# Four transformer layers on one core: the softmax of the first attention phase moves from ACT to Pool and behind the transposition

## The reference

```
x = x + L0_xattn(layernorm(x), ctx, ctx, mask0)     # 16 heads of 8, additive mask, relu(ctx @ wo + b)
x = x + L0_ffn(layernorm(x))                        # 8 experts of 512, the best 2 of each token
x = x + L1_xattn(layernorm(x), ctx, ctx, mask1)     # projections with bias, clip to +-100, mask
x = x + L1_ffn(layernorm(x))                        # gated, fake-quantised
x = x + L2_xattn(...); x = x + L2_ffn(...)          # attention; slots with a top-8 routing
x = x + L3_xattn(...); x = x + L3_ffn(...)          # attention with heads of 64; shared and 8 routed experts

scores  = einsum('bhqd,bhkd->bhqk', q, k) + mask
weights = softmax(scores)                           # exp(s - max) / sum
out     = einsum('bhqk,bhkd->bhqd', weights, v)
```

## Time and profile before

| | us |
|---|---|
| median of 3 runs | 2166.7 |
| lowest and highest run | 2157.89, 2175.78 |
| span of the profiled execution | 2161.6 |
| PE, DVE, ACT, POOL busy in the span | 1864.7, 1485.2, 1300.1, 616.4 |

### The profile page before, as it was taken

One profiled execution on the slowest core, in us unless ns is written; L12 is line 12 of the kernel. 1 busy time (PEld: TensorE's weight loads), 2 busy tenths in 40 slices (PEclk: granted clock), 3 DMA queues, 4 the chain that ended last, 5 costly groups with the idle time before them and its releaser, 6 DMA issues.

```text
span 2161.6 us, 49950 instructions
## 1 busy us (share of the span) xinstructions
PE 1864.7 (86%) x17665; PEld 1517.8 (70%) x17669; DVE 1485.2 (69%) x3873; ACT 1300.1 (60%) x4466; POOL 616.4 (29%) x610
## 2 busy tenths in 40 slices
PE   3987988888889999648788989999999998898878
PEld 2776877777778777536666667777787777676765
DVE  5887776786877888566776676776767565564456
ACT  1886655565556688436677766666666654554432
POOL 0003021241312230014343434244353533333221
PEclk9998999999999999867799999999999999999999
DMA  8013334463444310210000011232222223232351
GB/s 240 17 31 102 106 114 144 130 180 96 141 128 140 102 31 7 96 64 20 24 25 2 20 39 33 83 92 66 89 62 80 82 70 105 61 96 79 99 155 51
DMA packets 119637, 178.44 MB, mean 83 GB/s; under 512 B 9824, under 2 KB 77728, under 8 KB 119136
## 3 DMA queue, kind: packets, MB, share of 16 engines
q1 hardware_dynamic: 111712, 159.51, 24.6%
q0 software_dynamic: 7680, 15.74, 2.5%
HBM read 141.26 MB, written 33.95 MB: 81 GB/s over the span
## 4 chain that ended last, share of the span: by engine, by line
PE 37%; DVE 9%; ACT 5%; issue 4%; POOL 1%; DMA 0%; DVEq 0%; ACTq 0%; SPq 0%
PE ps L1659 5%; PE ps L1944 5%; PE ps L1892 3%; PE ps L1697 3%; PE ps L1885 3%; ACT pb L2093 2%; PE ps L1681 2%; PE ps L1866 2%; PE ps L1688 2%; PE ps L1670 2%; PE ps L1707 1%; DVE nm L2472 1%; PE ps L1715 1%; PE ps L1914 1%; PE ps L1858 1%
## 5 line engine op out<-in xcount | busy, mean ns | idle before, releaser
L2093 ACT ACTIVATE pb<-ps,nm 128x128 f32<-128x128 f32 x1024 | 363.2, 377 | 194.1 <-DVE nm L2472 194.0
L2141 POOL TENSOR_TENSOR pb<-pb,rcs 128x512 f32<-128x512 f32 x256 | 267.8, 1047 | 661.6 <-DVE rcs L2480 660.8
L981 ACT ACTIVATE pb<-pb,nm 128x128 f32<-128x128 f32 x1024 | 313.0, 393 | 52.1 <-DVE nm L1206 50.6
L2497 DVE COPY pt<-ps 128x512 f32<-128x512 f32 x128 | 88.2, 689 | 198.0 <-PE ps L1944 197.9
L2093 ACT ACTIVATION_READ_ACCUMULATOR pb<-ps,nm 128x1 f32 x1024 | 221.8, 217 | 0.0
L2472 DVE TENSOR_REDUCE nm<-ps 128x8 f32<-128x1024 f32 x128 | 155.8, 1217 | 61.9 <-PE ps L1892 38.7
L1944 PE MATMUL ps<-w,pb 128*128 128x128 f32 x1024 | 168.3, 290 | 21.4 <-ACT pt L2101 10.2
L1206 DVE TENSOR_REDUCE nm<-pb 128x8 f32<-128x1024 f32 x128 | 156.1, 1220 | 4.4
L1944 PEld LDWEIGHTS ps<-w,pb 128*128 128x128 f32 x1024 | 122.2, 148 | 45.1 <-ACT pt L2101 19.3
L865 PE MATMUL ps<-w,pb 128*128 128x128 f32 x1024 | 146.0, 286 | 6.8 <-ACT pb L981 6.6
L2101 ACT ACTIVATE pt<-ps 128x512 f32<-128x512 f32 x128 | 76.9, 601 | 92.9 <-PE ps L1944 92.8
(11 more groups left out here) (379 smaller groups left out, 4415.6 us busy)
## 6 DMA issues: line engine op xcount, KB each, us to landing
big<-in_we SPq DMA_DIRECT2D x92, 514.0 KB, 3.7
big<-in_we SPq DMA_DIRECT2D x109, 384.0 KB, 3.1
sorted_out<-big SPq DMA_DIRECT2D x27, 256.0 KB
big<-sorted_in SPq DMA_DIRECT2D x7, 960.0 KB, 5.8
sorted_in<-big SPq DMA_DIRECT2D x4, 1472.0 KB, 12.2
hidden<-h_all SPq DMA_DIRECT2D x7, 512.0 KB, 3.0
h_all<-hidden SPq DMA_DIRECT2D x7, 512.0 KB, 3.8
sorted_out<-h_all SPq DMA_DIRECT2D x14, 256.0 KB
```

The costliest lines, as they stand in the source:

```text
L981: m = a.activation(pb[:, n % 2, k * S:(k + 1) * S], pb[:, n % 2, k * S:(k + 1) * S], ACT.Exp, bias=nm[:, n % 2, k:k + 1])
L2093: m = a.activation(pb[:, n % 2, e * S:(e + 1) * S], ps[:, score_bank(n) + half, k * S:(k + 1) * S], ACT.Exp, bias=nm[:, n % 2, e:e + 1], a ...
L2141: g_.tensor_tensor(p4, p4, r4.unsqueeze(2).to_broadcast([P, 4, S]), ALU.mult).then_inc(n2["p_normed"], 1)
L2497: v.tensor_copy(pt[:, p % 2, 4 * S:8 * S], ps[:, BANK_T, :]).then_inc(n2["p_lo"], 1)
```

## The change

Pool adds the negative maximum to the scores in SBUF, in two halves of 4 matrices (`shift`), first thing in every turn of its loop. PE transposes these shifted scores as soon as a half is there. ACT takes the exponential while it copies the transposed matrices out of PSUM, for both halves and in all units; the 8 exponentials in SBUF are gone, and DVE no longer copies the lower half. The four masked copies of the queries move from DVE (place 3) to ACT (place 2). The gathers, all issued in unit 0 before, are issued 2, 3 and 3 at a time in units 0, 1 and 2; the scatters, 4 at a time in units 28 to 31 before (and the like 16 units later for each pair), 3 at a time in units 27 to 32, the last one alone. The identity products are gone.

```diff
-        IDLE_A = 3
+        GATHERS = {0: range(0, 2), 1: range(2, 5), 2: range(5, 8)}
+        SCATTERS = [range(3 * i, min(3 * i + 3, 2 * PB)) for i in range(6)]
+        SCATTERS_FROM = 3 * NU + 3
...
 @block.tensor
-                                if not k and not any(tiles_at(place, n) for place in range(3)):
-                                    for i in range(IDLE_A):
-                                        pe.matmul(ps[:, 2, i % 4 * P:(i % 4 + 1) * P], ident, ident, start=True, stop=True)
-                                pe.wait_ge(s["exps"], 2 * p + 1 + k // 4)
+                                pe.wait_ge(s["shifted"], 2 * p + 1 + k // 4)
...
 @block.scalar
+                    if layer == 0 and here == (2, 4):
+                        queries(j + 1, (front.yT_ready, g + 1), W("hm"))
+                    if layer == 1 and here == (2, 6):
+                        queries(j + 1, (s["q_col"], g + 1), W("hms"))
...
+                    for i in range(4):
+                        m = a.activation(qms[j % 2][:, i, :], qT[:, :], ACT.Copy, scale=heads_mask[:, i:i + 1])
+                    m.then_inc(s["q_ready"], 1)
...
-                        a.activation(pt[:, p % 2, 0:4 * S], ps[:, 2, :], ACT.Copy).then_inc(s["p_hi"], 1)
-                        if not any(tiles_at(place, n) for place in range(3)):
-                            a.wait_ge(s["transposed"], 2 * p + 2)
-                            a.activation(pt[:, p % 2, 4 * S:8 * S], ps[:, 3, :], ACT.Copy).then_inc(s["p_lo"], 1)
+                        a.activation(pt[:, p % 2, 0:4 * S], ps[:, 2, :], ACT.Exp).then_inc(s["p_hi"], 1)
+                        a.wait_ge(s["transposed"], 2 * p + 2)
+                        a.activation(pt[:, p % 2, 4 * S:8 * S], ps[:, 3, :], ACT.Exp).then_inc(s["p_lo"], 1)
                     work(1, n)
-                    if n < NUN:
-                        a.wait_ge(s["maxed"], n + 1)
-                        for k in range(BLK):
-                            m = a.activation(pb[:, n % 2, k * S:(k + 1) * S], pb[:, n % 2, k * S:(k + 1) * S], ACT.Exp,
-                                             bias=nm[:, n % 2, k:k + 1])
-                            if k % 4 == 3:
-                                m.then_inc(s["exps"], 1)
...
 @block.gpsimd
+                def shift(n):
+                    g_.wait_ge(s["maxed"], n + 1)
+                    for half in range(2):
+                        p4 = pb[:, n % 2, 4 * half * S:4 * (half + 1) * S].rearrange("p (k s) -> p k s", k=4)
+                        m4 = nm[:, n % 2, 4 * half:4 * half + 4]
+                        g_.tensor_tensor(p4, p4, m4.unsqueeze(2).to_broadcast([P, 4, S]), ALU.add)\
+                            .then_inc(s["shifted"], 1)
...
                 for n in range(NUN + 2 * NU):
                     j, u = divmod(n, NU)
+                    if n < NUN:
+                        shift(n)
                     layer, g = stream(j + 1)
-                    if layer == 1 and u == 0:
...
-                        for k in range(2 * G):
+                    if layer == 1 and u in GATHERS:
...
+                        for k in GATHERS[u]:
...
-                    if layer == 0 and g % 2 and u >= 4:
...
-                        for k in range(4 * (u - 4), 4 * (u - 3)):
+                    p, at = divmod(n - SCATTERS_FROM, 2 * NU)
+                    if 0 <= p < NP and at < len(SCATTERS):
...
+                        for k in SCATTERS[at]:
...
 @block.vector
-                    if layer == 0 and here == (3, 4):
-                        queries(j + 1, (front.yT_ready, g + 1), W("hm"))
-                    if layer == 1 and here == (3, 6):
-                        queries(j + 1, (s["q_col"], g + 1), W("hms"))
...
                         if n >= 2:
-                            v.wait_ge(s["exps"], 2 * (n - 1))
+                            v.wait_ge(s["shifted"], 2 * (n - 1))
...
-                    if 0 <= n - 1 < NUN and any(tiles_at(place, n) for place in range(3)):
-                        p = n - 1
-                        v.wait_ge(s["transposed"], 2 * p + 2)
-                        if p >= 2:
-                            v.wait_ge(s["pv"], p - 1)
-                        v.tensor_copy(pt[:, p % 2, 4 * S:8 * S], ps[:, 3, :]).then_inc(s["p_lo"], 1)
```

More of the change, by code:

```diff
@@ L298, in build @@
                       "p_lo", "pv", "o_recip", "normed", "oT_psum", "oT_ready", "out_psum", "bias_added"]
-        att_a = attention_sems("a", both_kinds + ["q_ready", "masked", "o_read", "o_turned"])
+        att_a = attention_sems("a", both_kinds + ["q_ready", "masked", "shifted", "o_read", "o_turned"])
         att_b = dict(att_a, **attention_sems("b", ["sums_turned", "p_normed", "k3_psum", "k3_col", "v_row", "chunk_added",
@@ L956, in work, with queries @@
                         tile(*item)
+                def queries(j, there, heads_mask):
+                    a.wait_ge(*there)
+                    if j >= 2:
+                        a.wait_ge(s["scores"], NU * (j - 1))
+                    for i in range(4):
+                        m = a.activation(qms[j % 2][:, i, :], qT[:, :], ACT.Copy, scale=heads_mask[:, i:i + 1])
+                    m.then_inc(s["q_ready"], 1)
                 a.wait_ge(front.yT_psum, 1)
                 a.activation(qT[:, :], ps[:, 6, :], ACT.Copy).then_inc(front.yT_ready, 1)
+                queries(0, (front.yT_ready, 1), W("hm"))
                 for n in range(NUN + 2 * NU):
@@ L1002, in _ @@
                     j, u = divmod(n, NU)
+                    if n < NUN:
+                        shift(n)
                     layer, g = stream(j + 1)
-                    if layer == 1 and u == 0:
[L1005 to L1008, removed]
-                        for k in range(2 * G):
+                    if layer == 1 and u in GATHERS:
+                        if u == 0:
+                            g_.wait_ge(moe["stored"], 16 * NQ0 * (g // 2 + 1))
+                            if g:
+                                g_.wait_ge(moe["gathered"], 16 * 2 * G * g)
+                                g_.wait_ge(moe["combined"], g)
+                        for k in GATHERS[u]:
                             e = k // G * PB + g % 2 * G + k % G
@@ L1025, in _ @@
                         pow_(last_ln if layer else experts, g + 1)
-                    layer, g = stream(j - 2)
-                    if layer == 0 and g % 2 and u >= 4:
-                        p = g // 2
-                        if u == 4:
+                    p, at = divmod(n - SCATTERS_FROM, 2 * NU)
+                    if 0 <= p < NP and at < len(SCATTERS):
+                        if at == 0:
                             g_.wait_ge(moe["index"], p + 1)
@@ L1050, in apply @@
                     layernorm_apply_dve(v, f, n)
[L1052 to L1058, removed]
                 def tile(g, kind, t):
@@ L1174, in _ @@
                 apply(front, 0, 1)
-                queries(0, (front.yT_ready, 1), W("hm"))
                 for n in range(NUN + 2 * NU):
```

## The result

The changed kernel takes 2222.9 us (median; 2216.1 to 2239.7) against 2171.2 (the kernel before, now with a fourth run): **slower**, ratio 1.0268 with its 95% interval [1.0213, 1.0324]. The forecast was 2177; the time is that of rival B (2222). The rest of the program, which the change leaves alone, took 1306 us in this execution and 1297 in the profiled one before, so 9 us of the 76 between the two spans don't come from the phase.

What follows compares the result with a forecast made beforehand. Only the first attention phase counted, PE its busiest engine, with waits ending mostly on DVE and DMA. Terms -7 - 10 - 12 + 17 + 4 + 11 + 15 + 10 - 18 = +10 gave 2177 us; full range 2118 to 2228.

Steps and rivals of the forecast that it cites:

- rival B: Slower: Pool's queue becomes the bound, DVE stands at the normalisation with PE idle; +55 us, 2222; chance 0.20.
- Pool beside DVE: DVE's side work behind each reduction slowed by Pool's shift, a third of 45 us counted: +15 (0 to +45).
- Pool's order: Shift ahead of Pool's other work in every unit delays layer-norm power, scatters and gathers: +17, +4 and +11 us.
- The power: Layer-norm power for the next group, unit 1 of seven streams, comes late and DVE waits: +17 (0 to +23).
- The reload: First pair's scatters end later between shifts, so PE's reload of sorted tokens comes later: +4 (-1 to +7).
- The gathers: Gathers between shifts delay the combined sum by 5.5 us in each of two streams without tiles: +11 (0 to +14).
- The gains: Savings in the first attention phase from undisturbed units, identity products, queries and tile stretch: -47 us together.
- the clock: Without identity products PE's clock falls about once more in each of five streams: +10 (0 to +90).
- The path of undisturbed units: Some 34 undisturbed units outside the tiles take 3.7 us against 3.9: -7 us.
- Queries: Masked query copies moved from DVE to ACT; seven disturbed units outside the tiles save 1.7 each: -12 (0 to -30).
- Identity products: Removed products no longer delay PE, counted for half of the 26 disturbed units: -10 (0 to -56).
- Tile stretch: Units 34 to 101, with expert tiles: DVE and ACT lose work, PE waits less: -18 (0 to -45).
- Rival C: Slower: PE's clock stays at 1.2 GHz outside the tiles, 60 units make +90: 2257; chance 0.06.

Runs made afterwards that it cites:

- x13: Changed kernel without the shift, with two idle Pool sums of 128x512 a unit in its place: 2214.9 us, ratio 1.0235 to the kernel before.
- x14: Changed kernel without the shift, with two idle Pool powers of 128x4 a unit in its place: 2184.3 us, ratio 1.0088 to the kernel before.
- x3: Changed kernel with Pool's front layer-norm power issued ahead of the shift: 2207.6 us, ratio 1.017 to the kernel before.
- x11: Changed kernel without the shift, the maximum formed and waited for but not subtracted: 2143.6 us, ratio 0.9868 to the kernel before.
- x9: Changed kernel with the masked query copies back on DVE: 2227.8 us, ratio 1.0264 to the kernel before.
- x8: Kernel before with only the masked query copies moved from DVE to ACT: 2189.6 us, ratio 1.0109 to the kernel before.
- x1: Changed kernel with the identity products put back in units without tiles: 2225.2 us, ratio 1.0265 to the kernel before.
- x5: Kernel before with two idle Pool powers of 128x4 added to each unit: 2174.3 us, ratio 1.0014 to the kernel before.
- x4: Kernel before with two idle Pool sums of 128x512 added to each unit: 2212.9 us, ratio 1.0192 to the kernel before.
- x2: Kernel before with only the identity products left out: 2175.5 us, ratio 1.0028 to the kernel before.

## Why the prediction was wrong

The mechanisms were the right ones; the sum failed in its sizes, all in one direction. Measured as steps, the +10 should have been -25 + 41 + 31 + 8 = +55 (the result itself is +52 on its own runs of the kernel before). I take the last step to the gains, since their term for the path had the shift in it.

- **Pool beside DVE, +15, measured 31: the step that failed, and the only one whose miss is clear of the noise by the medians and by the ratios alike.** "56 groups ... 45 us of DVE; most lies under PE, I count a third." The 45 us came out (45.0 measured), in part by luck: it is 47 rows with up to 2.4 us each, not 56 with 0.8. The third did not: x13 less x14 is 31 of 47.3, and in the kernel before 64 us of stretch cost 45. Both are some two thirds, the share of rival B. Units 14, 22, 104 and 112 show why: outside the tiles the side work stands right behind a reduction and ahead of the next unit's mask sum, on the chain that PE waits for, so covering it by PE's busy share was wrong.
- **Pool's order, 17 + 4 + 11 = +32, measured 41 (48 by the ratios).** The power is right (seven waits, 19.7 us; x3 gives 15). The reload is right (4 us more in x14). The gathers were too low: I had the streams with tiles "barely" covered, and in x14 the way from unit 67 to 68 is 7.3 and from 83 to 84 2.8 us longer than in x11, beside 6.1 and 6.0 behind units 107 and 115, the two I had counted.
- **The gains, -47 and +10 for the clock; -25 without the shift in x11, -17 with the last step.** The miss of 20 (16 by the ratios) is no smaller than the first, but the two steps together are uncertain by some 17. The path of undisturbed units is 3.7 us as forecast, but there are fewer of them: of the 57 ways between reductions outside the tiles 29 were under 4.3 us before and 13 are after. Queries -12: nothing that shows here (x9), +21 alone (x8); I had priced what DVE gains and not ACT's four copies, for which there was no row. Identity products -10 and clock +10: x1 puts both back and finds nothing, which is their sum as forecast; neither is shown by itself. Tile stretch -18: -8 in x11 (525.0 against 532.9), and +22 in the changed kernel, where PE's gap grew instead of closing by 15; a quarter of DVE's time was too much.

With 31 for the 15 alone the forecast would have been +26, half of what was measured; the rest is spread over two steps whose misses lie at the edge of the noise. Rival B had the terms nearly as measured: 43 for Pool's order, 30 for Pool beside DVE, -18 for the rest. (Inside Pool's order it had the power too high and the gathers too low.) I gave it 0.20; what I held against it, that three quarters of the phase's time has units of 4.6 us and more, says nothing of the units in which Pool is late. (The chances count a sixth of the forecast above 2188, the text beside them a quarter; the sum of 0.33 goes by the sixth.)

The rule of the Trainium skill ("SBUF — State Buffer", the part on its two sides) fits the stretched forms: normalisations, copies and products of two SBUF operands, not reductions, reciprocals or statistics (277 to 281 ns before and after). The trace agrees with it there: by it the groups that I counted were the right ones, and by the earlier trace rows alone they would have been fewer. In one thing the trace differs from the rule as the prediction gives it: a power of 128x4 is a Pool operation too and takes 1.02 us, but in x5 and x14 it locked none of these forms out (stretch 0.5 and 1.2 us). The measurement decides: the Pool operation matters as well as DVE's.

Rival C fell: the clock of the outer stretches was 0.78 and 0.82, not near 0.5, and x1 raised it with no gain in time. What the transposition alone does to the clock no run here shows.

What stays open: how much of the last 8 us is noise (0.5 us in each undisturbed unit is the part that the trace shows), what the queries, the identity products and the clock are worth one by one in the changed kernel, and whether the steps add up in another order.

## What to carry to other kernels

Pool sums of 128x512 were paid by DVE, not by Pool: list DVE's operations that would run beside such work, and count their stretch by where they stand, in full between two operations of the critical chain, and not by the busy share of another engine. Pool runs in order, so an operation that waits for something late belongs behind the small work that others need early. And two of the eight blocks on Pool, with the rest left where there was room and Pool's small work in front, did better than all eight.

## What the runs showed of the hardware

- Two idle Pool sums of 128x512 a unit cost 45 us (x4), two idle powers of 128x4 3 [-1, 7] (x5, ratio 1.0014 [0.9994, 1.0034]), though they hold Pool about as long (257.7 us of the middle stretch in x14 and 259.1 with sums in x13).
- Even a DVE operation on 128x4 is held: in the changed kernel 0.17 us became 0.70 on average and up to 0.92. DVE operations that read PSUM weren't: the relu of the expert tiles (line 1073) took 0.344 us beside a sum and elsewhere.
- An ACT copy of 128x512 from SBUF with a scale took 0.714 us, one from PSUM 0.60; DVE's had a mean of 0.477 in the kernel before.
- The granted clock of the first stretch fell from 0.96 to 0.85 (x2) and 0.88 (x11) at 9 us more and 8.5 us less time: it doesn't tell the time by itself.
